# A five-stage LayerNorm whose scales are computed inside each stage, and the state space's output bias added beside the gates

## The chip, the cores and the metric

One Trainium2 chip; the kernel runs on one core. The metric is the device time of the whole kernel in microseconds; lower is better. Engines: PE is TensorE (matrix products), DVE is VectorE, ACT is ScalarE, POOL is GpSimd, SP issues transfers.

## The reference

An x of 16 x 64 tokens by 512 features goes through six blocks, each `x = x + block(layernorm(x))`; the layernorm has no weights:

```python
def _layernorm(x, axis=-1, eps=1e-05):
    m = jnp.mean(x, axis=axis, keepdims=True)
    v = jnp.var(x, axis=axis, keepdims=True)
    return (x - m) / jnp.sqrt(v + eps)
...
    x = x + _L0_xattn_ref(_layernorm(x, axis=-1), ctx_512, ctx_512, ...)   # 16 heads, 1601 keys a sequence
    x = x + _L0_attn_ref(_layernorm(x, axis=-1), ...)                      # state space, gate, output projection + b_out
    x = x + _L0_ffn_ref(_layernorm(x, axis=-1), ...)                       # router keeps 4 of 16 blocks a token
    x = x + _L1_xattn_ref(_layernorm(x, axis=-1), ctx_512, ctx_512, ...)   # one head, width 512
    x = x + _L1_attn_ref(_layernorm(x, axis=-1), ...)                      # causal self-attention
    x = x + _L1_ffn_ref(_layernorm(x, axis=-1), ...)                       # 4-bit weights, 16-bit activations
```

## The kernel before, in words

x lies in SBUF as eight tiles of 128 tokens by 512 (`NT` = 8, `x[:, t, :]`). The program is a row of stages, each a block of five instruction streams, one per engine; a stage begins on every engine when all have ended the one before. The stages are `cross0` (first cross-attention), `state_space`, `block_ffn`, `cross1_queries` and `cross1_batches` (second cross-attention), `self1`, and `quant_ffn`. Inside a stage the order of each engine's work is written out by hand, with semaphores between engines.

**The layernorm between stages.** Each of the first five blocks ends with an add per tile into x on VectorE, followed by that tile's statistics (`tile_stats`, L77: `bn_stats` into `k.stats`). When seven tiles are counted, and before the wait for the eighth tile's product, VectorE runs `norm_scales(0, 7)` (L82): seven `bn_aggr`, epsilon added, then 1/sqrt by an integer seed and three Newton steps of three small operations each, all on VectorE, and a last one for the shift -mean/sqrt. This stands in `cross0_batches` at L925, `state_space` at L1287, `block_ffn` at L1633, `cross1_batches` at L1904, `self1` at L2080. The next stage normalizes tiles at once (`hat_on_vector`, L187); after the fourth it runs `norm_scales` again for the eighth tile alone (`last_scales_on_vector`, L159; 14 operations). In `SharedNorm` (cross1_queries, self1) and in quant_ffn ScalarE normalizes tiles 4 to 7 from shift and scale. TensorE then turns each normalized tile (four transpositions into a PSUM bank, `turn_on_tensor`), and ScalarE or VectorE copies it out as xT. The norm at the very start of the program is another one (`small_on_vector`, L163, with the root on ScalarE, `root_on_scalar`, L210); its `loaded` is set.

**state_space.** VectorE: norm, then per tile the evictions of the projections; cumulative sums; a loop of 8 steps in which TensorE makes one product of the last eight Cm projections and one gate product a step, ScalarE evicts the projections and VectorE the gate (L1256; two banks); then 32 units (tile, head group). In unit n TensorE makes the decay and score products, ScalarE the exponential, VectorE `gated(n - 3)` (L1262) and `mixed(n)` (L1271, two operations), TensorE the products with the mixed matrix. In units 4 to 11 VectorE also adds the output bias `bO` to one tile of x (L1281). Last, eight output products (L1190), each added into x (L1289). GpSimd and SP, from the last gate on (`s_gT`), split the weights of block_ffn into two bf16 parts in 16 pieces (L1046, L1048) and store them.

The transfers of a stage's weights are issued by SP when the stage starts. In state_space TensorE waits for them before the first projections (`s_w`), in block_ffn after two turnings (`s_in`), in self1 before the queries and keys (`s_in`).

A table load of ScalarE (another set of functions for root, exponential, Silu or sigmoid) is put by the compiler directly ahead of the first activation that needs it, and ahead of that activation's wait.

## Time and profile before

| | us |
|---|---|
| three runs | 1679.1, 1680.76, 1686.83 (median 1680.76) |
| the profiled execution | 1682.18 |
| its span | 1680.5 |
| PE busy | 1549.7 (92%) |
| DVE busy | 1195.5 (71%) |
| ACT busy | 878.2 (52%) |
| POOL busy | 723.9 (43%) |

| stage | starts at, us into the span |
|---|---|
| cross0 | 0 |
| state_space | 854.7 |
| block_ffn | 995.4 |
| cross1_queries | 1212.5 |
| cross1_batches | 1238.1 |
| self1 | 1371.2 |
| quant_ffn | 1430.7 |

The profile's span is what the profiler saw between first and last instruction; the execution's own time lies 1.7 us above it. An engine's busy share says nothing of who waits: that is in the timeline, where a row gives the start, the length, the engine, the line, the operation and, in brackets, how long the engine had been idle before it and who ended that. Rows of one form that follow each other closely are merged (x2, x8).

### The profile page before, as it was taken

The page shows a single profiled execution, that of the slowest core. Times are in us where ns is not written, and L with a number is a line of the kernel's source. Part 1 is how long each engine was busy: PE and PEld are TensorE (multiplying, and loading weights), DVE is VectorE, ACT ScalarE, POOL GpSimd, SP SyncE. Part 2 cuts the span into 40 slices and gives each one's busy share as a digit, 9 for nine tenths or more (in the row PEclk, how much of TensorE's full clock was granted, in tenths as well). Part 3 has the DMA queues.
Part 4 walks back from the last instruction along what each step waited for, and adds up shares of the span by engine and source line. Part 5 has one row for each costly group of instructions (what it writes and reads, how often), then busy time and mean ns, then how long its engine had stood idle before and what let it go on. Part 6 is the DMA issues. An engine that isn't in the chain of part 4 may idle for free. (4 is left out here: it accounts for less than half of the span.)

```text
span 1680.5 us, 33759 instructions
## 1 busy us (share of the span) xinstructions
PE 1549.7 (92%) x13881; PEld 811.9 (48%) x13990; DVE 1195.5 (71%) x2049; ACT 878.2 (52%) x1176; POOL 723.9 (43%) x348
## 2 busy tenths in 40 slices
PE   6999999999999999999878889999889989899469
PEld 3445555555555555555453545344535544444134
DVE  6688888888888888888566558998832244527981
ACT  1387777777777777777544213431112221327650
POOL 1467888888887888876404832330000000000000
PEclk9999999999999999999989989999999999899779
DMA  3489999999999999999923644669699942000001
GB/s 139 126 181 194 186 195 191 189 199 185 196 189 199 190 194 188 188 201 166 195 87 107 222 167 150 158 165 213 177 421 416 377 181 127 1 0 1 0 1 51
DMA packets 554667, 282.02 MB, mean 168 GB/s; under 512 B 481664, under 2 KB 532608, under 8 KB 551440
## 3 DMA queue, kind: packets, MB, share of 16 engines
q1 hardware_dynamic: 554512, 279.84, 70.4%
q8 instruction: 111, 1.82, 0.4%
q14 instruction: 44, 0.36, 0.1%
HBM read 138.74 MB, written 22.54 MB: 96 GB/s over the span
## 5 line engine op out<-in xcount | busy, mean ns | idle before, releaser
L604 POOL TENSOR_TENSOR x<-x_prob,x 128x1604 bf16<-128x1604 f32 x120 | 387.9, 3232 | 144.0 <-ACT x L769 144.0
L899 DVE TENSOR_REDUCE x_negmax<-x_score 128x1 f32<-128x1604 f32 x128 | 233.7, 1826 | 17.5 <-PE x_score L645 7.3
L759 ACT ACTIVATE x_prob<-x_score,x_negmax 128x1604 f32<-128x1604 f32 x128 | 204.8, 1600 | 25.7 <-DVE x_negmax L899 21.0
L628 PE MATMUL x_ring<-x_ctx_hi,wk_split 128*128 128x400 bf16 (+1 forms) x1024 | 216.2, 333 | 0.3 <-DVE x_kT L827 0.3
L628 PE MATMUL x_ring<-wv_split,x_ctx_hi 128*128 128x512 bf16 (+1 forms) x770 | 200.3, 379 | 9.7 <-issue 6.9
L827 DVE SCALAR_TENSOR_TENSOR x_kT<-x_ring,bk,x_kT 128x400 bf16<-128x400 f32 (+1 forms) x256 | 162.3, 635 | 31.7 <-ACT x_kT L748 23.9
L769 ACT CAST x<-x_prob 128x1604 bf16<-128x1604 f32 x120 | 183.0, 1525 | 0.0
L833 DVE TENSOR_TENSOR x_v<-x_ring,x_v 128x512 bf16<-128x512 f32 (+1 forms) x208 | 143.8, 691 | 52.8 <-ACT x_v L752 50.0
L748 ACT ACTIVATE x_kT<-x_ring,bk 128x400 bf16<-128x400 f32 (+1 forms) x196 | 116.5, 594 | 90.7 <-PE x_ring L628 89.8
L752 ACT CAST x_v<-x_ring 128x512 bf16<-128x512 f32 (+1 forms) x148 | 86.7, 586 | 97.0 <-PE x_ring L628 97.0
L628 PEld LDWEIGHTS x_ring<-x_ctx_hi,wk_split 128*128 128x128 bf16 x1024 | 93.8, 97 | 87.0 <-issue 19.4
L2274 POOL MEMSET g_round<- 128x1 f32 x1 | 0.1, 98 | 300.8 <-POOLq L1927 300.8
L628 PE MATMUL x_ring<-x_ctx_lo,wk_split 128*128 128x400 bf16 (+1 forms) x512 | 128.4, 332 | 0.0
L628 PEld LDWEIGHTS x_ring<-wv_split,x_ctx_hi 128*128 128x128 bf16 (+1 forms) x832 | 77.4, 99 | 102.2 <-DVE x_kT L827 9.3
L661 PEld LDWEIGHTS x_pv<-x_pT,x_v 128*64 128x64 bf16 (+1 forms) x3328 | 97.6, 110 | 59.2 <-issue 58.5
L661 PE MATMUL x_pv<-x_pT,x_v 128*64 128x128 bf16 (+1 forms) x3328 | 118.3, 222 | 8.0 <-DMA x_pT<-x_kT 5.7
L2300 PE MATMUL g_bank<-g_x_split,g_w 128*128 128x512 bf16 x564 | 123.7, 379 | 1.4 <-DVE g_x_split L2413 0.8
L628 PE MATMUL x_ring<-wv_split,x_ctx_lo 128*128 128x512 bf16 (+1 forms) x415 | 123.5, 379 | 0.1
L553 POOL TENSOR_TENSOR x_ctx_lo<-x_stage,x_ctx_hi 128x802 bf16<-128x802 f32 (+1 forms) x64 | 106.1, 1658 | 30.2 <-DVE x_ctx_hi L808 28.9
L645 PE MATMUL x_score<-x_kT,x_q_rows 32*64 32x400 bf16 (+1 forms) x3072 | 91.6, 336 | 0.7 <-ACT x_prob L759 0.7
L546 POOL TENSOR_TENSOR x_ctx_hi<-x_stage,x_zero 128x800 bf16<-128x800 f32 (+1 forms) x60 | 91.2, 1521 | 0.3 <-DMA x_stage<-in_ctxT 0.2
L1435 PE MATMUL f_bank<-f_x_split,f_w 128*128 128x512 bf16 x374 | 89.3, 386 | 0.8 <-issue 0.4
(305 smaller groups left out, 2398.1 us busy)
## 6 DMA issues: line engine op xcount, KB each, us to landing
y_ctx<-in_ctx SPq DMA_DIRECT2D x16, 1664.0 KB, 12.3
y_ctxT<-in_ctxT SPq DMA_DIRECT2D x16, 1601.0 KB, 19.5
x_stage<-in_ctxT SPq DMA_DIRECT2D x48, 400.0 KB, 4.6
x_q_rows<-q_rows SPq DMA_DIRECT2D x64, 128.0 KB, 3.1
m_xT<-in_L_ffn_w SPq DMA_DIRECT2D x16, 512.0 KB, 4.6
ffn_w_parts<-m_xT SPq DMA_DIRECT2D x32, 256.0 KB, 2.7
x_stage<-in_ctxT SPq DMA_DIRECT2D x16, 401.0 KB, 4.7
f_w<-ffn_w_parts SPq DMA_DIRECT2D x4, 1024.0 KB, 8.4
```

What stands on the lines that cost most here:

```text
L553: pool.tensor_tensor(clo[:, :, at], stage[:, c % 2, :, 0:n], chi[:, :, at], ALU.subtract).then_inc(clo_done, 1)
L604: pool.tensor_tensor(ph[:, g % 2, 1, 0:NKP], prob[:, g % 2, :], ph[:, g % 2, 0, 0:NKP], ALU.subtract).then_inc(pl_done, 1)
L628: last = pe.matmul(out_, lhs, rhs, start=(i == 0), stop=(i == len(steps) - 1))
L645: last = pe.matmul(score[L * u:L * u + L, 512 * c:512 * c + w], qp[rows, par, a, hq, p // 2, :], kT[rows, par, hk, p // 2, QW * c:QW * c + w],
L661: last = pe.matmul(pv[L * h:L * h + L, 0:2 * L], v[0:kw, vpar, t, 2 * pp + h, :, :].rearrange("p s d -> p (s d)"), pT[0:kw, u, :, t, L * h ...
L748: nc.scalar.activation(kT[:, par, 0, m, n0:n0 + w], ring[g % RING][:, 0:w], ACT.Identity, bias=bk[:, KD * turned(c) + m:KD * turned(c) + m ...
L759: nc.scalar.activation(prob[:, g % 2, :].rearrange("p (c n) -> p c n", n=QW), scores, ACT.Exp, bias=nmax[:, g % 2:g % 2 + 1], accum_out=rs ...
L769: nc.scalar.copy(ph_of[g >= LAST][:, g % 2, 0, 0:NKP], prob[:, g % 2, :]).then_inc(ph_done, 1)
L827: dve.scalar_tensor_tensor(kT[:, par, 1, m, n0:n0 + w], ring[g % RING][:, 0:w], bk[:, KD * turned(c) + m:KD * turned(c) + m + 1], kT[:, pa ...
L833: dve.tensor_tensor(v[0:kw, par, m, :, 1, :], ring[g % RING][0:kw, :].rearrange("p (h d) -> p h d", h=H), v[0:kw, par, m, :, 0, :], ALU.su ...
L899: dve.tensor_reduce(nmax[:, pair % 2:pair % 2 + 1], scores, mybir.AxisListType.XY, ALU.max, negate=True).then_inc(max_done, 1)
L2300: last = pe.matmul(banks[2 + n % NB_G][:], wt[:, hw, j, m * P:(m + 1) * P], xs[:, hx, j, 512 * c:512 * c + 512], start=(i == 0 and j == 0) ...
```

## The change

Two things, and no others.

1. `norm_scales` is gone, and with it the scales of seven tiles at the end of a stage and of the eighth inside the next. The five stages after cross0 now begin as the norm at the start of the program does: `small_on_vector` on VectorE (eight `bn_aggr`, epsilon, reciprocal of ScalarE's root, four operations of one Newton step), with `root_on_scalar` on ScalarE; in `SharedNorm` and quant_ffn one more operation makes the shift of all tiles. The tiles are normalized after that. `tile_stats` stays where it was.
2. In state_space the eight adds of `bO` move from units 4 to 11 to the gate loop, one behind each gate's eviction.

The diff, cut:

```diff
-    def norm_scales(self, dve, first, last, step, base):
...
     def on_vector(self, dve):
+        self.small_on_vector(dve)
+        self.hat_on_vector(dve, range(NT))
+
+    def small_on_vector(self, dve):
+        before = NT if self.loaded else 0
         if self.loaded:
-            self.small_on_vector(dve)
-            self.hat_on_vector(dve, range(NT))
-        else:
-            self.hat_on_vector(dve, range(NT // 2))
-            self.last_scales_on_vector(dve)
-            self.hat_on_vector(dve, range(NT // 2, NT))
...
     def root_on_scalar(self, nc, act):
-        if not self.loaded:
-            return
         act.wait_ge(self.s_var, 1)
         nc.scalar.activation(self.small[:, 1, :], self.small[:, 0, :], ACT.Sqrt).then_inc(self.s_root, 1)
...
     def on_scalar(self, nc, act):
+        self.root_on_scalar(nc, act)
+        act.wait_ge(self.s_shift, 1)
         for t in range(self.HALF, NT):
-            if t == NT - 1:
-                act.wait_ge(self.s_var, self.LAST_SCALES)
             nc.scalar.activation(self.xhat[:, t, :], self.x[:, t, :], ACT.Identity, bias=self.shift[:, t:t + 1],
...
     def on_vector(self, dve):
+        self.small_on_vector(dve)
+        dve.scalar_tensor_tensor(self.shift[:], self.meanvar[:, :, 0], -1.0, self.rstd[:, :, 0], ALU.mult,
+                                 ALU.mult).then_inc(self.s_shift, 1)
         self.hat_on_vector(dve, range(self.HALF))
-        self.last_scales_on_vector(dve)
...
                 dve.tensor_scalar(gT[:, n // 2, 512 * (n % 2):512 * (n % 2) + 512], banks[4 + n % 2],
                                   bG[:, n // 2:n // 2 + 1], None, ALU.add).then_inc(s_gT, 1)
+                dve.tensor_tensor(x[:, n, :], x[:, n, :], bO[:], ALU.add).then_inc(s_xo, 1)
...
                 mixed(n)
-                if 4 <= n < 4 + NT:
-                    dve.tensor_tensor(x[:, n - 4, :], x[:, n - 4, :], bO[:], ALU.add).then_inc(s_xo, 1)
...
             for t in range(NT):
-                if t == NT - 1:
-                    k.norm_scales(dve, 0, NT - 1, s_stats, NT - 1)
                 dve.wait_ge(s_xo, NT)
...
+            norm.root_on_scalar(nc, act)
             for c in range(2):
                 for t in range(6 * c, 2 * c + 6):
                     norm.turned_on_scalar(nc, act, t)
```

The last piece is block_ffn's ScalarE. The call of `norm_scales` at the last tile goes in the same way in the four other stages, and quant_ffn's streams are changed as SharedNorm's.

**Where instructions stand now.** VectorE at the end of cross0 and the start of state_space, before (the add L932 is the last tile's, in two halves; L347 and L1220 are the branch between the stages):

```order
L845 TENSOR_TENSOR x<-x,x_stage 128x512
L88 BN_AGGR x_meanvar<-x_stats 128x2 x7
L91 TENSOR_SCALAR x_meanvar<-x_meanvar 128x7
...
L106 SCALAR_TENSOR_TENSOR x_shift<-x_meanvar,x_rstd 128x7
L932 TENSOR_TENSOR x<-x_ring,x 128x256 x2
L80 BN_STATS x_stats<-x 128x6
L347 UNCONDITIONAL_BRANCH
L1220 UNCONDITIONAL_BRANCH
L189 TENSOR_SCALAR m_xhat<-x,x_meanvar,x_rstd 128x512 x4
L88 BN_AGGR x_meanvar<-x_stats 128x2
```

and with the change:

```order
L809 TENSOR_TENSOR x<-x,x_stage 128x512
L894 TENSOR_TENSOR x<-x_ring,x 128x256 x2
L78 BN_STATS x_stats<-x 128x6
L312 UNCONDITIONAL_BRANCH
L1181 UNCONDITIONAL_BRANCH
L134 BN_AGGR m_meanvar<-x_stats 128x2 x8
L137 TENSOR_SCALAR m_small<-m_meanvar 128x8
L139 RECIPROCAL m_small<-m_small 128x8
L142 TENSOR_TENSOR m_small<-m_small 128x8
L144 TENSOR_TENSOR m_small<-m_small 128x8
L146 TENSOR_SCALAR m_small<-m_small 128x8
L148 TENSOR_TENSOR m_rstd<-m_small 128x8
```

The block between the seventh tile's add and the eighth's has gone; fourteen operations plus the root stand ahead of the first normalized tile. The same holds at the four other seams.

VectorE in state_space, gate loop and first units, before:

```order
L1252 TENSOR_SCALAR m_minus<-m_cum 80x512
L1256 TENSOR_SCALAR m_gT<-m_banks,m_bG 128x512 x8
L1271 TENSOR_TENSOR m_mix<-m_decay,m_banks 128x2x128 x6
L1262 TENSOR_TENSOR m_xhat<-m_banks,m_gT 128x128
L1271 TENSOR_TENSOR m_mix<-m_decay,m_banks 128x2x128 x2
L1262 TENSOR_TENSOR m_xhat<-m_banks,m_gT 128x128
L1271 TENSOR_TENSOR m_mix<-m_decay,m_banks 128x2x128 x2
L1281 TENSOR_TENSOR x<-x,m_bO 128x512
```

and with the change (the pair L1217, L1219 comes eight times):

```order
L1213 TENSOR_SCALAR m_minus<-m_cum 80x512
L1217 TENSOR_SCALAR m_gT<-m_banks,m_bG 128x512
L1219 TENSOR_TENSOR x<-x,m_bO 128x512
...
L1219 TENSOR_TENSOR x<-x,m_bO 128x512
L1233 TENSOR_TENSOR m_mix<-m_decay,m_banks 128x2x128 x6
L1224 TENSOR_TENSOR m_xhat<-m_banks,m_gT 128x128
L1233 TENSOR_TENSOR m_mix<-m_decay,m_banks 128x2x128 x2
```

The add stands behind each gate's eviction, and between a mixing and the next gated product nothing is left.

ScalarE in self1, before (L266 normalizes tiles 4 to 7, L2044 is the exponential):

```order
L266 ACTIVATE sn_xhat<-x,x_shift,x_rstd 128x512 x4
L270 COPY s_xT<-s_bank 128x4x128 x3
L2039 COPY s_v<-s_bank 128x512
L2044 ACTIVATE s_prob,s_stat<-s_sc,s_stat 128x128 x4
L2039 COPY s_v<-s_bank 128x512
```

and with the change:

```order
L176 ACT_TABLE_LOAD
L176 ACTIVATE sn_small<-sn_small 128x8
L229 ACTIVATE sn_xhat<-x,sn_shift,sn_rstd 128x512 x4
L233 COPY s_xT<-s_bank 128x4x128 x3
L1991 COPY s_v<-s_bank 128x512
L1996 ACT_TABLE_LOAD
L1996 ACTIVATE s_prob,s_stat<-s_sc,s_stat 128x128 x4
```

A load stands ahead of the root at the stage's start and another ahead of the first exponential. In the whole program ScalarE has 5 loads before and 13 with the change.

## Rows read from the trace of the kernel before

**Rows 1.** Timeline of VectorE, unit loop (start us, us, engine, line, operation, [idle before <- releaser]).
```profile
909.56 0.75 DVE L1271 TENSOR_TENSOR m_mix<-m_decay,m_banks 128x256 f32<-128x256 f32 x2 [0.81 <-PE m_banks L1179]
...
931.01 0.75 DVE L1271 TENSOR_TENSOR m_mix<-m_decay,m_banks 128x256 f32<-128x256 f32 x2 [0.46 <-PE m_banks L1179]
...
961.00 0.75 DVE L1271 TENSOR_TENSOR m_mix<-m_decay,m_banks 128x256 f32<-128x256 f32 x2 [0.81 <-PE m_banks L1179]
```

**Rows 2.** By line: two adds of one form (ns min/median/max, first and last start us).
```profile
L1281 DVE TENSOR_TENSOR x<-x,m_bO x8: 1517/1754/2147, 910.2 to 927.7; 128x512 f32<-128x512 f32 x8
...
L1730 DVE TENSOR_TENSOR x<-x,yq_bv x8: 681/687/689, 1220.1 to 1228.8; 128x512 f32<-128x512 f32 x8
```

**Rows 3.** Timeline of VectorE, last step of the gate loop.
```profile
900.44 0.75 DVE L1256 TENSOR_SCALAR m_gT<-m_banks,m_bG 128x512 f32<-128x512 f32 x1 [1.32 <-PE m_banks L1118]
```

**Rows 4.** Stretches: us, PE busy, PEld, DVE, ACT, POOL, granted clock, DMA share, GB/s.
```profile
862.00:864.00 2.00, 2.00 (x12) 2.00 (x11) 0.77 (x2) 0.43 (x1) 0.00 (x0) 0.50 0.89 278
...
880.00:900.00 20.00, 18.61 (x100) 4.44 (x96) 9.73 (x16) 14.38 (x24) 0.00 (x0) 1.00 0.00 1
```

**Rows 5.** Timeline, norm at the start of the program.
```profile
11.68 0.64 DVE L170 BATCH_NORM_AGGREGATE x_prob<-x_prob 128x2 f32<-128x6 f32 x8
...
12.73 0.21 ACT L214 ACTIVATE x_prob<-x_prob 128x8 f32<-128x8 f32 x1 [10.66 <-DVE x_prob L173]
...
14.02 3.74 DVE L189 TENSOR_SCALAR x_v<-x_v,x_prob 128x512 f32<-128x512 f32 x8
```

**Rows 6.** Timeline of ScalarE, a table load in state_space.
```profile
866.28 1.28 ACT L1198 ACT_TABLE_LOAD   x1
...
867.58 0.63 ACT L1198 ACTIVATE m_xn<-m_xb 128x512 f32<-128x512 f32 x1
```

**Rows 7.** Timeline, end of cross0 and start of state_space.
```profile
846.58 3.70 PE L679 MATMUL x_ring<-wo,catT 128*128 128x512 f32 x8
...
852.91 0.74 DVE L932 TENSOR_TENSOR x<-x_ring,x 128x256 f32<-128x256 f32 x2
...
854.68 0.33 SPq L1052 DMA_DIRECT2D m_wXA<-in_L_attn_WXA  x1
...
860.55 2.13 PE L1103 MATMUL m_banks<-m_wXA,m_xT 128*128 128x132 f32 x8 [2.94 <-DMA m_wG<-in_L_attn_WG]
```

**Rows 8.** Timeline, end of state_space and start of block_ffn.
```profile
975.53 16.90 PE L1190 MATMUL m_banks<-m_wO,m_xhat 128*128 128x512 f32 x39
...
993.66 0.68 DVE L1289 TENSOR_TENSOR x<-x,m_banks 128x512 f32<-128x512 f32 x1
...
995.36 0.39 SPq L1374 DMA_DIRECT2D f_router<-in_L_ffn_router_w  x1
...
1000.71 0.72 PEld L201 LDWEIGHTS f_bank<-ident,f_h 128*128 128x128 f32 x4 [3.14 <-DMA f_sel<-head_picks]
```

**Rows 9.** Timeline, start of cross1_queries (TensorE turns tiles 6 and 7).
```profile
1217.98 1.23 PE L258 MATMUL yq_bank<-ident,yq_xhat 128*128 128x128 f32 x8 [0.33 <-ACT yq_xhat L266]
```

**Rows 10.** Timeline, end of cross1_batches and start of self1.
```profile
1367.17 1.96 PE L1852 MATMUL y_wout<-y_wv,y_oT 128*128 128x512 f32 x4 [0.51 <-issue]
...
1369.20 0.68 DVE L1906 TENSOR_TENSOR x<-x,y_wout 128x512 f32<-128x512 f32 x1
...
1371.19 0.38 SPq L1961 DMA_DIRECT2D s_wq<-in_L_attn_Wq  x1
...
1378.27 0.30 PEld L1973 LDWEIGHTS s_bank<-s_xT,s_wq 128*128 128x128 f32 x2 [2.86 <-DMA s_wv<-in_L_attn_Wv]
```

**Rows 11.** Timeline, end of self1 and start of quant_ffn.
```profile
1425.86 0.58 DVE L88 BATCH_NORM_AGGREGATE x_meanvar<-x_stats 128x2 f32<-128x6 f32 x7
...
1428.98 0.74 DVE L2082 SCALAR_TENSOR_TENSOR x<-s_bank,s_stat,x 128x512 f32<-128x512 f32 x1
...
1430.77 1.92 DVE L189 TENSOR_SCALAR g_up<-x,x_meanvar,x_rstd 128x512 f32<-128x512 f32 x4 [0.32 <-PEq L1927]
...
1435.31 4.48 DVE L2402 TENSOR_REDUCE g_amax<-g_up 128x4 f32<-128x2048 f32 x2
```

More of the change, by code:

```diff
@@ L55, in __init__ @@
         self.used = []
-        self.stats = self.meanvar = self.rstd = self.shift = None
+        self.stats = None
         self.x = None
@@ L75, in sem, with tile_stats @@
         return self.used[-1]
-    def tile_stats(self, dve, x, t, done, counted):
+    def tile_stats(self, dve, x, t, done):
         dve.wait_ge(*done)
-        dve.bn_stats(self.stats[:, t, :], x[:, t, :]).then_inc(counted, 1)
-    def norm_scales(self, dve, first, last, step, base):
-        ve, r, u = self.meanvar[:, first:last, 1], self.rstd[:, first:last, 0], self.shift[:, first:last]
-        if base:
-            dve.wait_ge(step, base)
-        for t in range(first, last):
-            dve.bn_aggr(self.meanvar[:, t, :], self.stats[:, t, :]).then_inc(step, 1)
-        done = base + last - first
-        dve.wait_ge(step, done)
-        dve.tensor_scalar(ve, ve, EPS, None, ALU.add).then_inc(step, 1)
-        dve.wait_ge(step, done + 1)
-        dve.tensor_scalar(r.bitcast(I32), ve.bitcast(I32), 1, None, ALU.logical_shift_right).then_inc(step, 1)
-        dve.wait_ge(step, done + 2)
-        dve.tensor_scalar(r.bitcast(I32), r.bitcast(I32), -1.0, ROOT_SEED, ALU.mult, ALU.add).then_inc(step, 1)
-        done += 3
-        for _ in range(3):
-            dve.wait_ge(step, done)
-            dve.scalar_tensor_tensor(u, r, -0.5, r, ALU.mult, ALU.mult).then_inc(step, 1)
-            dve.wait_ge(step, done + 1)
-            dve.tensor_tensor(u, u, ve, ALU.mult).then_inc(step, 1)
-            dve.wait_ge(step, done + 2)
-            dve.scalar_tensor_tensor(r, u, 1.5, r, ALU.add, ALU.mult).then_inc(step, 1)
-            done += 3
-        dve.wait_ge(step, done)
-        dve.scalar_tensor_tensor(u, self.meanvar[:, first:last, 0], -1.0, r, ALU.mult, ALU.mult).then_inc(step, 1)
+        dve.bn_stats(self.stats[:, t, :], x[:, t, :])
     def keep_busy(self, pe, ident, bank, count):
@@ L129, in __init__ @@
         self.loaded = loaded
-        self.k = k
         if home is None:
-            self.meanvar, self.rstd = k.meanvar, k.rstd
+            self.stats = k.sb(ctx, name + "_stats", [P, NT, 6]) if loaded else k.stats
+            self.meanvar = k.sb(ctx, name + "_meanvar", [P, NT, 2])
+            self.rstd = k.sb(ctx, name + "_rstd", [P, NT, 1])
+            self.small = k.sb(ctx, name + "_small", [P, 4, NT])
         else:
@@ L146, in __init__ @@
         self.s_xT = k.sem(ctx, name + "_xT_done")
[L148 removed]
     def on_vector(self, dve):
+        self.small_on_vector(dve)
+        self.hat_on_vector(dve, range(NT))
+    def small_on_vector(self, dve):
+        before = NT if self.loaded else 0
         if self.loaded:
[L152 to L168 removed]
+            for t in range(NT):
+                dve.wait_ge(*self.loaded(t))
+                dve.bn_stats(self.stats[:, t, :], self.x[:, t, :]).then_inc(self.s_stats, 1)
+            dve.wait_ge(self.s_stats, before)
         for t in range(NT):
@@ L2322, in _ @@
         def _(act):
+            act.wait_ge(norm.s_var, 1)
+            nc.scalar.activation(norm.small[:, 1, :], norm.small[:, 0, :], ACT.Sqrt).then_inc(norm.s_root, 1)
+            act.wait_ge(s_shift, 1)
             for t in range(NT // 2, NT):
-                if t == NT - 1:
-                    act.wait_ge(norm.s_var, norm.LAST_SCALES)
-                nc.scalar.activation(xhat[:, t, :], x[:, t, :], ACT.Identity, bias=k.shift[:, t:t + 1],
+                nc.scalar.activation(xhat[:, t, :], x[:, t, :], ACT.Identity, bias=shift[:, t:t + 1],
                                      scale=norm.rstd[:, t, :]).then_inc(s_hat2, 1)
```

49 lines of the change are left out of this document (13 added, 36 removed).

## The prediction

> **What bounds the kernel now.** I read the busy shares first, then for each stage that the change touches the timeline around its start and end, and asked who waits for whom there. The first 854 us (cross0) run as before up to their last microseconds, so only five seams between stages and one loop are at stake.
>
> The loop is state_space's unit loop. From unit 13 on, two units' first mixings stand 1.765 us apart: (961.00 - 931.01) / 17 [rows 1]. There VectorE waits 0.81 us per unit for TensorE, so TensorE sets the pace. Between unit 4 (909.56) and unit 13 (931.01), where each of eight units carries one add of the output bias, nine units take 21.45 us in place of 9 x 1.765 = 15.88, and the idle time in front of the mixing is gone: there VectorE sets the pace. The add is why. It takes 1.5 to 2.1 us, while an add of the same form in cross1 takes 0.69 [rows 2]. In the unit loop GpSimd is splitting the next stage's weights nearly without a pause, and both of the add's sources lie in SBUF; in cross1 GpSimd is idle.
>
> At a seam the reader is to see two things: whether the last add of a stage starts when its product is there or only when the block of 7-tile scales is done, and what the first product of the next stage waits for.
>
> **The bias adds.** Out of the unit loop they give back 21.45 - 15.88 = 5.6 us. In the gate loop each follows a gate's eviction of 0.75 us, before which VectorE waits 1.32 us [rows 3]: the step is 2.07 us long, and 0.75 + 0.69 fits with 0.63 to spare. GpSimd is busy 0.00 us there [rows 4], so 0.69 is the price to take. Were it the 1.75 of the unit loop, the step would grow by 0.43 us, 3.4 us in eight; that is the bound above. The eighth add lies beside ScalarE's table load and first exponential. The block of splitting on GpSimd starts with the last gate, as before, and by the timeline its last stores are out while TensorE still works on the output products, so 5.6 us less do not uncover it. I take -5.6; from -5.6 + 3.4 = -2.2 to -6.
>
> **What replaces the scales.** Each of five stages now begins with all eight aggregates, one add, a square root on ScalarE behind a table load, a reciprocal and four small steps before its first normalized tile. The same chain at the start of the program takes 14.02 - 11.68 = 2.34 us, with the root 1.05 us after the first aggregate [rows 5]; the table was there long before. A load takes 1.28 us and the next activation follows 0.02 us behind it [rows 6]. The load stands ahead of the wait, so it starts with the stage and holds the root back to 1.3 us: 2.34 + 0.26 = 2.6 us to the first tile. In the three stages that share the tiles with ScalarE, one more small step makes 2.8: five of them fill 14.02 - 12.73 - 0.21 = 1.08 us [rows 5], 0.2 each. Below, nothing is shorter than 2.34; above, a load wholly in line gives 2.34 + 1.28 = 3.6. I take 2.6 and 2.8.
>
> The Trainium skill (ScalarE: Activation LUTs, section What ACT_TABLE_LOAD costs) puts a drain of about 1.38 us beside each load, 2.66 us per switch. No drain follows the load in rows 6; by that rule the first tile would come at 4.0.
>
> Three more loads, for the exponentials of block_ffn, cross1 and self1, have cover: softmax's mask is ready before TensorE comes to it, ScalarE is idle at the start of the batches, and in self1 TensorE turns the probabilities only after four products of values. Zero for these; if the cover were gone, 1.28 each. On ScalarE that makes eight loads more.
>
> **Seam A, cross0 to state_space.** The last product ends at 846.58 + 3.70 = 850.28, its add starts at 852.91 [rows 7], because the scale block stands ahead of it. Without the block it starts 0.1 behind the product: -2.5. The stage starts at 854.68, and its first projection waits until 860.55 for weights whose transfers start with the stage: 5.9 us. The new chain needs 2.6 to the first tile, 0.5 to write it (3.74 / 8 [rows 5]), at most 1.2 to turn it (two tiles take 1.23 at full clock [rows 9], so one takes as much at half) and at most 0.7 to copy it: 5.0 us, under 5.9. So the whole -2.5 stays, and its other bound is -2.5 + 1.3, should the chain take longer than the transfer by as much as a load.
>
> **Seam B, state_space to block_ffn.** The last product ends at 975.53 + 16.90 = 992.43, its add starts at 993.66 [rows 8]: -1.1. The third turning waits for a transfer until 1000.71, 5.35 us after 995.36. In the new order it also needs the first tile turned and copied twice: 2.6 + 0.5 + 1.2 + 1.2 = 5.5. I add 0.1: -1.0.
>
> **Seam C, block_ffn to cross1.** The last product of block_ffn is a long one, and its add already waits for it, so the block was hidden: 0 gained. At the start of cross1_queries, TensorE has nothing until the first tile, and its eight turnings lead straight to the products, with no transfer in the way. First tile +2.8; the wait of 0.33 us for tile 7, whose scales came late [rows 9], falls away: +2.4. In the batches TensorE never waits for the context, so nothing further on takes this back.
>
> **Seam D, cross1 to self1.** The last product ends at 1367.17 + 1.96 = 1369.13, its add starts at 1369.20 [rows 10]: the block ended just in time, 0 gained. The stage starts at 1371.19, and its first products wait until 1378.27 for a transfer, 7.1 us in. With the new chain the four tiles that they need are copied at 2.8 + 1.9 + 3 x 0.7 = 6.8: 0.
>
> **Seam E, self1 to quant_ffn.** Here the block is bare: it starts at 1425.86, when VectorE could have taken the last add, which starts at 1428.98 [rows 11]: -3.1. Then the peak of all tiles starts 1435.31 - 1430.77 = 4.5 us after the first tile; in the new order it follows four tiles (1.92) behind 2.8, at 4.7. Together -2.9.
>
> **Sum**: -5.6 - 2.5 - 1.0 + 2.4 + 0 - 2.9 = -9.6 us. The profiled execution took 1682.2 us, so 1672.6 in its terms; it lies 1.4 above the median of the three runs, 1680.8, so I predict 1671.2. About 0.5% (8.4 us) is what a measurement of this kernel tells from no change, so "faster" begins below 1672.4, hardly above my number.
>
> **Rivals.**
>
> *The load costs more than its row.* If ScalarE stays shut for as long again as the load lasted, 1.28 us, the first tile comes 1.3 later. Seam A then has 5.0 + 1.3 = 6.3 against 5.9 (+0.4), B, C and E take +1.3 each, D 8.1 against 7.1 (+1.0): +5.3, giving 1676.5. Against it stand rows 6; for it, that no row shows a load between a barrier and a root. The skill's drain, named above, is this rival, and would give much the same. Chance 0.10.
>
> *TensorE's clock.* It is at 0.50 of full, 1.2 GHz, when state_space's first projections run [rows 4], though TensorE is fully busy there; a wait of 2.94 us lies before them [rows 7]. In block_ffn too the turnings follow such a wait. The new chain makes the gap ahead of the turnings longer but nearly closes the one behind them, so the clock may come back sooner in A and B, and later in C. A tile's projections take 2.13 us at half clock [rows 7], of which full clock saves half: two tiles each in A and B give -4; two tiles' worth lost in C or E gives +2. That is 1667 to 1673. Chance of the gain 0.14; the loss lies within my range.
>
> *The start of a stage is bare everywhere.* If in A, B and D not the transfers but the new chain sets the first product (transfers land earlier, or turnings are slower than I take), the chain costs 2.6 + 2.6 + 2.8 + 2.8 + 2.8 = 13.6; against it stand 5.6 for the adds and 2.5 + 1.1 + 3.1 = 6.7 for the blocks: +1.3 us, 1682.1, slower. With 1.28 more at each, 1688.5. It decides from the point at which the first tile's copy ends after the transfer lands, 5.9 us into state_space. What speaks against it are the waits for transfers in rows 7, 8 and 10. Chance 0.06.
>
> *The adds do not leave the path.* If GpSimd's splitting or something else, and not VectorE, set the slow units, or the adds stretch the gates by 3.4, the -5.6 shrinks to 0 or -2.2: 1676.8 or 1674.6. The 0.81 us of idle that return as soon as the adds end speak against it. Chance 0.08.
>
> **How the numbers follow.** The forecast has 0.62 and an own range of 1667.5 to 1675: each seam is read to about 0.5 us, the run to run spread of 1679.1 to 1686.8 adds two. It splits 0.40 faster, 0.22 same. The rivals give 0.14 faster; 0.10, 0.08 and half of 0.06 same; the rest slower. So faster 0.54, same 0.43, slower 0.03. The range 1666 to 1677.5 takes in the clock's gain, the dear load and the stretched gates.
>
> **What would show it.** In the new profile the add with m_bO lasts 0.69 us and all units are 1.77 apart; the last adds of cross0 and self1 start within 0.2 of their product or of a free VectorE; the root follows the start of a stage by 1.3 us; the first projection of state_space still waits for its transfer; cross1_queries' first turning comes 3.4 us into its stage. A step of the gate loop over 2.1 us, a first tile later than 3 us, or a first projection released by a copy would prove me wrong in that term.

## The result, and the profile after

The changed kernel takes 1669.98 us (median of five runs, 1667.66 to 1672.3) against 1680.76 us before; the ratio is 0.9936, 95% interval 0.9919 to 0.9954. That is 10.8 us less, 7.7 to 13.6 by the interval. Forecast were 1671.2 us and 9.6 us less.

The two profiled executions lie 14.6 us apart (spans 1680.5 and 1665.9), because the one of before is among the longer of its runs and the one after the shortest of its own. Cut at the stages' starts, they show where the difference comes from:

| stretch | before, us | after, us | difference | forecast |
|---|---|---|---|---|
| cross0 to the end of its last product | 850.28 | 846.84 | -3.44 | 0, no edit there |
| from there to the start of state_space | 4.40 | 1.87 | -2.53 | -2.5 |
| state_space | 140.68 | 133.81 | -6.87 | -5.6 - 1.1 |
| block_ffn | 217.18 | 217.75 | +0.57 | +0.1 |
| cross1_queries | 25.53 | 27.29 | +1.76 | +2.4 |
| cross1_batches | 133.12 | 133.38 | +0.26 | 0 |
| self1 | 59.54 | 56.04 | -3.50 | -3.1 |
| quant_ffn | 249.77 | 248.92 | -0.85 | +0.2 |

(A stage's start is the issue of its first transfer, in quant_ffn GpSimd's first instruction; the end is the page's span, which is given to 0.1 us.) The first row is taken as scatter: in the thirteen profiles of this case the end of cross0's last product lies between 846.5 and 850.3 us, and TensorE's last wait for a transfer in cross0 is 5.49 us in the kernel before, 3.89 in the changed one and 4.92 in old_C, which ends cross0 as the changed one does. The three profiles with the old end of cross0 lie in the upper half, at 848.6 to 850.3, the ten with the new one at 846.5 to 848.8; that the edit has no part in this is not shown. Without that row the profiles differ by 11.2 us.

**Seam A.** Timeline of the changed kernel (start us, us, engine, line, operation, [idle before <- releaser]), end of cross0 and start of state_space, which answers to [rows 7]:

```profile
843.14 3.70 PE L643 MATMUL x_ring<-wo,catT 128*128 128x512 f32 x8
...
846.95 0.76 DVE L894 TENSOR_TENSOR x<-x_ring,x 128x256 f32<-128x256 f32 x2 [0.63 <-PE x_ring L643]
...
848.71 1.28 ACT L176 ACT_TABLE_LOAD   x1 [6.07 <-PEq L312]
...
850.00 0.21 ACT L176 ACTIVATE m_small<-m_small 128x8 f32<-128x8 f32 x1
...
851.29 3.74 DVE L153 TENSOR_SCALAR m_xhat<-x,m_meanvar,m_rstd 128x512 f32<-128x512 f32 x8
...
853.01 0.59 ACT L181 COPY m_xT<-m_banks 128x512 f32<-128x512 f32 x1 [2.80 <-PE m_banks L165]
...
853.87 0.59 ACT L181 COPY m_xT<-m_banks 128x512 f32<-128x512 f32 x1 [0.27 <-PE m_banks L165]
854.44 1.82 PEld L1064 LDWEIGHTS m_banks<-m_wXA,m_xT 128*128 128x128 f32 x8 [1.01 <-DMA m_wG<-in_L_attn_WG]
854.44 2.13 PE L1064 MATMUL m_banks<-m_wXA,m_xT 128*128 128x132 f32 x8 [0.61 <-ACT m_xT L181]
```

The last product ends at 843.14 + 3.70 = 846.84 and its add follows 0.1 later, where before it stood 2.6 behind [rows 7]. The load starts with the stage, at 848.71; the root follows at 850.00, 1.29 us in, and the first tile at 851.29, 2.58 in. The first projection starts 5.73 in, against 5.87 before. TensorE's row names the copy of the second tile, the weight loader's row the transfer of m_wG. It was the transfer: the first projection needs only the first tile, whose copy ends at 853.60, 0.84 us earlier, and the copy that TensorE's row names ends at 854.46, just behind the projection's start. The run own_waits below confirms it.

Stretches of the same kernel, the columns as in [rows 4]: the first projection, and a stretch that holds the third and those behind it.

```profile
854.44:856.56 2.12, 2.12 (x9) 2.12 (x10) 0.59 (x2) 0.01 (x1) 0.00 (x0) 0.50 0.79 156
...
858.70:868.00 9.30, 8.39 (x79) 7.96 (x84) 4.62 (x12) 7.29 (x13) 0.00 (x0) 1.00 0.21 80
```

TensorE's granted clock is 0.50 (1.2 GHz) at the first projection, as before, and 1.00 from 858.70.

**The bias adds.** Timeline of VectorE, a step of the gate loop and the mixings of two units; below, all adds by line (ns min/median/max):

```profile
881.87 0.75 DVE L1217 TENSOR_SCALAR m_gT<-m_banks,m_bG 128x512 f32<-128x512 f32 x1 [0.65 <-PE m_banks L1079]
882.53 0.68 DVE L1219 TENSOR_TENSOR x<-x,m_bO 128x512 f32<-128x512 f32 x1
...
910.48 0.75 DVE L1233 TENSOR_TENSOR m_mix<-m_decay,m_banks 128x256 f32<-128x256 f32 x2 [0.81 <-PE m_banks L1140]
...
912.25 0.75 DVE L1233 TENSOR_TENSOR m_mix<-m_decay,m_banks 128x256 f32<-128x256 f32 x2 [0.81 <-PE m_banks L1140]
```

```profile
L1219 DVE TENSOR_TENSOR x<-x,m_bO x8: 681/682/684, 880.5 to 895.0; 128x512 f32<-128x512 f32 x8
```

The add takes 0.68 us in every step. From the third mixing to the last of the 32 they stand 1.76 us apart, each behind a wait of 0.81 for TensorE.

**Seam B.** End of state_space, start of block_ffn ([rows 8] before):

```profile
957.82 22.91 PE L1151 MATMUL m_banks<-m_wO,m_xhat 128*128 128x512 f32 x53
...
980.84 0.69 DVE L1247 TENSOR_TENSOR x<-x,m_banks 128x512 f32<-128x512 f32 x1 [2.02 <-PE m_banks L1151]
...
988.32 1.12 PE L165 MATMUL f_bank<-ident,f_h 128*128 128x128 f32 x4 [0.64 <-DMA f_sel<-head_picks]
```

The product ends at 980.73, the add starts at 980.84, and the stage starts 1.1 us sooner behind the product than before (982.52 - 980.73 = 1.79 against 2.93). The third turning comes 5.80 us into the stage against 5.35.

**Seam C.** Start of cross1_queries ([rows 9] before):

```profile
1200.27 1.28 ACT L176 ACT_TABLE_LOAD   x1 [9.74 <-PEq L90]
...
1201.56 0.21 ACT L176 ACTIVATE yq_small<-yq_small 128x8 f32<-128x8 f32 x1
...
1202.93 1.91 DVE L153 TENSOR_SCALAR yq_xhat<-x,yq_meanvar,yq_rstd 128x512 f32<-128x512 f32 x4
...
1203.53 5.36 PE L221 MATMUL yq_bank<-ident,yq_xhat 128*128 128x128 f32 x32 [8.29 <-DVE yq_xhat L153]
...
1208.73 10.46 PE L1655 MATMUL yq_bank<-yq_xT,wqk 128*128 128x512 f32 x24
```

The root stands 1.29 us in, the first tile 2.66, the first turning 3.26 and the first product 8.46; before, that product stood 6.63 in. The 32 transpositions take 5.36 us here, at a mean granted clock of 0.67.

**Seams D and E.** self1's first queries ([rows 10]), and the last adds of self1 with quant_ffn's peak ([rows 11]):

```profile
1367.78 3.70 PE L1925 MATMUL s_bank<-s_xT,s_wq 128*128 128x512 f32 x8 [0.68 <-DMA s_wv<-in_L_attn_Wv]
```

```profile
1413.86 0.75 DVE L2032 SCALAR_TENSOR_TENSOR x<-s_bank,s_stat,x 128x512 f32<-128x512 f32 x1 [2.29 <-PE s_bank L1956]
1414.64 0.69 DVE L78 BATCH_NORM_STATS2 x_stats<-x 128x6 f32<-128x512 f32 x1
1415.25 0.73 DVE L2032 SCALAR_TENSOR_TENSOR x<-s_bank,s_stat,x 128x512 f32<-128x512 f32 x1
...
1421.67 4.48 DVE L2357 TENSOR_REDUCE g_amax<-g_up 128x4 f32<-128x2048 f32 x2
```

The queries start 6.84 us into self1 and wait for the transfer of s_wv, as before (7.08). The last add stands directly behind the statistics of tile 6, where before 3.1 us of small operations stood. The peak starts 4.69 us into quant_ffn, against 4.58.

### The profile page after: what moved, and what is told of

Read it like the earlier page. It is cut to its first block and busy times, and to the rows that moved or that the text cites. A ratio compares the mean times of both kernels' runs of the same rounds, so it can differ in the third digit from the quotient of the medians.

```text
span 1665.9 us, 33782 instructions
## 1 busy us (share of the span) xinstructions
PE 1558.5 (94%) x13990; PEld 809.1 (49%) x13990; DVE 1171.7 (70%) x1952; ACT 889.4 (53%) x1189; POOL 721.9 (43%) x348
## 5 line engine op out<-in xcount | busy, mean ns | idle before, releaser
L592 PE MATMUL x_ring<-wv_split,x_ctx_hi 128*128 128x512 bf16 (+1 forms) x832 | 214.2, 380 | 0.0
```

The costliest lines, as they stand in the source:

```text
L592: last = pe.matmul(out_, lhs, rhs, start=(i == 0), stop=(i == len(steps) - 1))
```

## The experiments

Each run gives a ratio to the kernel before, measured beside it, and a profile. Single executions of one kernel lie 2 to 10 us apart, so a single seam is read from the lengths of the stages:

| kernel | ratio, 95% interval | state_space | block_ffn | cross1_queries | self1 | quant_ffn |
|---|---|---|---|---|---|---|
| before | | 140.68 | 217.18 | 25.53 | 59.54 | 249.77 |
| changed | 0.9936 (0.9919-0.9954) | 133.81 | 217.75 | 27.29 | 56.04 | 248.92 |
| adds_only | 0.9968 (0.9955-0.9982) | 135.17 | 215.50 | 25.52 | 59.35 | 248.45 |
| scales_only | 0.9964 (0.9951-0.9978) | 139.48 | 216.99 | 28.02 | 56.60 | 251.25 |
| old_C | 0.9920 (0.9902-0.9938) | 134.15 | 217.23 | 25.52 | 59.30 | 248.59 |
| warm | 0.9932 (0.9914-0.9949) | 133.81 | 217.46 | 27.14 | 56.54 | 250.83 |
| more_loads | 0.9980 (0.9965-0.9995) | 134.61 | 217.40 | 29.90 | 57.28 | 253.19 |
| split_late | one run | 143.42 | 216.74 | 25.52 | 63.04 | 251.09 |
| own_waits | 0.9902 (0.9880-0.9923) | 131.77 | 215.90 | 27.53 | 55.69 | 251.51 |
| busy | 0.9912 (0.9891-0.9932) | 132.44 | 218.32 | 27.88 | 56.28 | 251.32 |
| changed_again | 0.9928 (0.9910-0.9947) | 134.01 | 216.85 | 27.82 | 55.98 | 249.12 |
| own_old | 0.9907 (0.9887-0.9928) | 131.66 | 217.91 | 25.51 | 55.68 | 251.27 |
| all_four | 0.9902 (0.9882-0.9922) | 131.27 | 217.43 | 25.52 | 55.30 | 249.24 |

**adds_only: the bias adds alone.**

```diff
@@ kernel before, state_space, VectorE
+                dve.tensor_tensor(x[:, n, :], x[:, n, :], bO[:], ALU.add).then_inc(s_xo, 1)
...
-                if 4 <= n < 4 + NT:
-                    dve.tensor_tensor(x[:, n - 4, :], x[:, n - 4, :], bO[:], ALU.add).then_inc(s_xo, 1)
```

> The kernel before with only the eight adds of the output bias moved into the gate loop; all scales stay as they were. Theory (VectorE paced units 4 to 12 because the add took 1.75 us beside GpSimd's splitting): 5.6 us faster than before, units 1.765 us apart throughout, the add 0.69 us, the gate step still 2.07. Rival (the scales made the whole difference, or the adds cost the gate loop what they give the unit loop): 0 to 2.2 us.

Measured: ratio 0.9968, 5.4 us less than before. state_space is 5.51 us shorter. The other stages have no edit, yet block_ffn, at 215.50, is the shortest of the thirteen profiles, 1.7 us under before, and quant_ffn is 1.3 us under before; no edit explains either. By line (ns min/median/max):

```profile
L1258 DVE TENSOR_TENSOR x<-x,m_bO x8: 680/681/681, 885.0 to 899.5; 128x512 f32<-128x512 f32 x8
```

The 5.6 us of the first term are there, and come from this edit alone.

**scales_only: the new norm alone.**

```diff
@@ changed kernel, state_space, VectorE
-                dve.tensor_tensor(x[:, n, :], x[:, n, :], bO[:], ALU.add).then_inc(s_xo, 1)
...
+                if 4 <= n < 4 + NT:
+                    dve.tensor_tensor(x[:, n - 4, :], x[:, n - 4, :], bO[:], ALU.add).then_inc(s_xo, 1)
```

> The changed kernel with the eight adds back in units 4 to 11; the new norm at the start of the five stages stays. Theory: seams A -2.5, B -0.7, C +1.8, D -0.2, E -3.1 and a little clock in quant_ffn, together 4 to 5 us faster than before, 5.6 us slower than the changed kernel. Rival (the adds are worth nothing): as fast as the changed kernel, 10.8 us faster than before.

Measured: ratio 0.9964, 6.1 us less than before (3.7 to 8.2 by the interval); 4 to 5 were expected. state_space is 1.20 us shorter than before, which is seam B's end without the adds. The two parts add up: 5.4 + 6.1 = 11.5 against 10.8 for the whole change, so neither hides the other.

**split_late: why the add was slow.** The kernel before, with one more wait on GpSimd.

```diff
@@ kernel before, state_space, GpSimd
             pool.wait_ge(s_gT, 2 * KD)
+            pool.wait_ge(s_xo, NT)
```

> The kernel before, its adds in units 4 to 11, but GpSimd's splitting of the next stage's weights begins only when the eighth add is done. Theory (the add is slow only because GpSimd works beside it): the add takes 0.69 us and nine units from unit 4 take 16 us in place of 21.45; the splitting then ends later than the stage's products, so the stage as a whole is longer, and block_ffn waits. Rival (the add is slow because of where it stands, or something other than GpSimd): it still takes 1.5 to 2.1 us.

Measured: all eight adds by line, then VectorE's timeline from the mixing of unit 4 to that of unit 13.

```profile
L1282 DVE TENSOR_TENSOR x<-x,m_bO x8: 682/684/686, 909.6 to 921.9; 128x512 f32<-128x512 f32 x8
```

```profile
908.90 0.75 DVE L1272 TENSOR_TENSOR m_mix<-m_decay,m_banks 128x256 f32<-128x256 f32 x2 [0.81 <-PE m_banks L1180]
909.57 0.68 DVE L1282 TENSOR_TENSOR x<-x,m_bO 128x512 f32<-128x512 f32 x1
...
924.78 0.75 DVE L1272 TENSOR_TENSOR m_mix<-m_decay,m_banks 128x256 f32<-128x256 f32 x2 [0.81 <-PE m_banks L1180]
```

At its old place, in the unit loop, the add takes 0.68 us once GpSimd is quiet, and nine units take 924.78 - 908.90 = 15.88 us, as the prediction had it for units without adds. The place was not at fault. The stage as a whole is 2.7 us longer than before, since the splitting, begun later, then ends last in it; the single run took 1688.6 us.

What happens in the collision is in the kernel before's timeline of unit 4 (GpSimd's L1046 and L1048 are the splitting):

```profile
909.36 1.90 POOL L1046 TENSOR_TENSOR m_xT<-m_xT,m_zero_col 128x1024 bf16<-128x1024 f32 x1
...
909.56 0.75 DVE L1271 TENSOR_TENSOR m_mix<-m_decay,m_banks 128x256 f32<-128x256 f32 x2 [0.81 <-PE m_banks L1179]
...
910.23 1.58 DVE L1281 TENSOR_TENSOR x<-x,m_bO 128x512 f32<-128x512 f32 x1
...
911.34 2.46 POOL L1048 TENSOR_TENSOR m_xT<-m_xT 128x1024 bf16<-128x1024 f32 x1
```

The add starts at 910.23, under a GpSimd operation that ends at 911.26, and lasts until 911.81, 0.55 us beyond that end. The same holds for all eight adds of this kernel:

| the add, start to end | GpSimd's running operation ends at | the add ends behind it by |
|---|---|---|
| 910.23 to 911.81 | 911.26 | 0.55 |
| 912.59 to 914.35 | 913.79 | 0.55 |
| 915.13 to 917.28 | 916.73 | 0.55 |
| 918.06 to 919.81 | 919.26 | 0.55 |
| 920.59 to 922.11 | 921.56 | 0.55 |
| 922.89 to 924.65 | 924.10 | 0.55 |
| 925.43 to 926.95 | 926.40 | 0.55 |
| 927.73 to 929.49 | 928.93 | 0.55 |

Whatever its length, an add ends at one distance behind GpSimd's operation. So it waits for that operation to finish; if both ran at half speed, the distance would vary. It works in the other direction too: GpSimd's next operation starts at 911.34, while the add still runs, and lasts 2.46 us, where in split_late this form takes 2.13 on average. The mixings, which have one of their two inputs in PSUM, take 0.75 us a pair beside GpSimd as without it. The Trainium skill (SBUF — State Buffer, section SBUF: two separate sides) has the rule: an operation of VectorE with two inputs in SBUF and a GpSimd operation that reads SBUF lock the same pair of ports, one for its whole length while the other is blocked. The rows above agree, with the one distance of 0.55 us in eight adds.

**old_C: seam C as before.** The functions `norm_scales` and the eighth tile's scales are taken back for this seam only.

```diff
@@ changed kernel, block_ffn and cross1_queries
+                if t == NT - 1:
+                    k.norm_scales(dve, 0, NT - 1, s_stats, NT - 1)
...
-        norm = SharedNorm(k, ctx, "yq", x, ident, banks[0:2] + banks[4:8], xT)
+        norm = SharedNorm(k, ctx, "yq", x, ident, banks[0:2] + banks[4:8], xT, early=True)
```

> The changed kernel with only the seam block_ffn to cross1_queries as before: seven tiles' scales under the last long product of block_ffn, the eighth's inside the stage, no root and no table load there. Theory (this seam alone loses): cross1_queries 25.5 us long in place of 27.3, 1.8 us faster than the changed kernel, so 12.6 us faster than before. Rival (a later wait takes it back, TensorE's clock or the batches' transfers): no faster than the changed kernel.

Measured: cross1_queries takes 25.52 us, as before, where the five profiles with the new chain and its one load have 27.3 to 28.0. The ratio is 0.9920, 2.7 us under the changed kernel's; the intervals overlap, so it is the stage's length that shows it. block_ffn did not grow (217.23): its end has more cover than the long product. In the kernel before, VectorE's last statistics end at 1209.40 and the last store of prepared weights lands at 1210.63; cross1_queries starts 1.9 us behind that landing, here and in eleven of the twelve other profiles. The profile would be faster still, had not self1 taken 59.30 us; its first queries, and the stretch in which they run:

```profile
1368.41 5.40 PE L1970 MATMUL s_bank<-s_xT,s_wq 128*128 128x512 f32 x8 [2.25 <-DMA s_wv<-in_L_attn_Wv]
```

```profile
1368.41:1371.90 3.49, 3.49 (x5) 1.48 (x6) 0.00 (x0) 0.00 (x0) 0.00 (x0) 0.62 1.01 437
```

The queries started behind the transfer of s_wv 8.40 us into self1, 1.6 later than in the changed kernel's profile, though nothing there differs; TensorE had waited 2.25 us, its clock in the stretch is 0.62, and the eight products take 5.40 us in place of 3.70 [rows 10].

**warm: the root's table already loaded.**

```diff
@@ changed kernel, end of ScalarE's work in cross0, state_space, block_ffn, cross1_batches, self1
+            nc.scalar.activation(k.warm[:], ident[:, 0:1], ACT.Sqrt)
```

> The changed kernel with a root of one column at the end of ScalarE's work in each of five stages, so that the table of the root is there when the next stage starts. Theory: the root follows the stage's start by 0.9 us (eight aggregates 0.64, the add 0.17, 0.05 between) in place of 1.3, so the first tile comes 0.4 us earlier; this is worth 0.4 each in cross1_queries and quant_ffn and nothing in state_space, block_ffn and self1, where a transfer ends last: 0.8 us faster than the changed kernel. Rival (the chain ends last at all five): 2.0 us faster. Rival (a load has a hidden cost after it, so the price seen is not all): more than 2.

Measured: timeline of cross1_queries, which starts at 1201.82, and of state_space's first projection (stage start 850.55).

```profile
1202.73 0.21 ACT L180 ACTIVATE yq_small<-yq_small 128x8 f32<-128x8 f32 x1 [9.17 <-DVE yq_small L141]
...
1204.10 1.91 DVE L157 TENSOR_SCALAR yq_xhat<-x,yq_meanvar,yq_rstd 128x512 f32<-128x512 f32 x4
```

```profile
856.47 2.13 PE L1069 MATMUL m_banks<-m_wXA,m_xT 128*128 128x132 f32 x8 [1.34 <-DMA m_wG<-in_L_attn_WG]
```

The root follows 0.91 us into the stage, the first tile 2.28: 0.38 earlier than in the changed kernel. In state_space the first projection still starts 5.92 in, released by the transfer, after 1.34 us of waiting in place of 0.61. cross1_queries is 0.15 us shorter, and in quant_ffn the first product of the hidden layer comes 15.19 in, against 15.57. Expected were 0.8 us in all; the ratio, 0.9932, cannot tell so little from nothing. The rival with five bare chains is out: in state_space, block_ffn and self1 a transfer released TensorE as before (5.92, 5.28 and 7.34 us in).

**more_loads: two table loads ahead of the root.**

```diff
@@ changed kernel, ScalarE, ahead of the root's wait in the five stages
+            nc.scalar.activation(k.warm[:, 0:1], ident[:, 0:1], ACT.Silu)
+            nc.scalar.activation(k.warm[:, 1:2], ident[:, 0:1], ACT.Sqrt)
```

> The changed kernel with an activation of one column from another table (Silu) and one from the root's table at the start of each of the five stages: two table loads ahead of the root in place of one. Theory (a load is its 1.28 us and an activation its 0.2, nothing hidden): the root waits until 1.28 + 0.2 + 1.28 + 0.2 = 3.0 us in, the first tile comes 1.7 us later; cross1_queries and quant_ffn grow by 1.7 each, state_space, block_ffn and self1, whose transfers land 0.5 to 1 us after the chain, by 0.9 to 1.7 each: 6 to 8 us slower than the changed kernel. Rival (each load leaves ScalarE shut for about as long again): the root at 5.5 us in, some 15 us slower.

Measured: ScalarE in cross1_queries.

```profile
1202.66 1.28 ACT L82 ACT_TABLE_LOAD   x1 [9.73 <-PEq L95]
1203.95 0.20 ACT L82 ACTIVATE warm<-ident 128x1 f32<-128x1 f32 x1
1204.16 1.28 ACT L83 ACT_TABLE_LOAD   x1
1205.45 0.20 ACT L83 ACTIVATE warm<-ident 128x1 f32<-128x1 f32 x1
1205.56 0.19 ACT L184 ACTIVATE yq_small<-yq_small 128x8 f32<-128x8 f32 x1
```

Load, activation, load, activation follow each other at 0.01 us; the root stands 2.90 us in. The ratio is 0.9980, 7.4 us above the changed kernel's (the medians lie 9.3 apart), and 6 to 8 were forecast. Part of that agreement is luck: cross1_queries grows by 2.6 and quant_ffn by 4.3 where 1.7 each were forecast, and TensorE's clock has its share in quant_ffn (last section); state_space grows by 0.8, self1 by 1.2, block_ffn not at all. What the run shows without luck is the timeline: each load has its own 1.28 us and nothing behind it.

**own_waits: TensorE waits only for what it uses.**

```diff
@@ changed kernel
-            sp.dma_start(wXA[:], d["L0_attn_WXA"]).then_inc(s_w, 16)
+            sp.dma_start(wXA[:], d["L0_attn_WXA"]).then_inc(s_wx, 16)
...
-            pe.wait_ge(s_w, 16 * 6)
+            pe.wait_ge(s_wx, 16)
...
-            sp.dma_start(wv[:], ...).then_inc(s_in, 16)
+            sp.dma_start(wv[:], ...).then_inc(s_wvin, 16)
...
-            pe.wait_ge(s_in, 48)
+            pe.wait_ge(s_in, 32)
```

TensorE waits for the other five weights of state_space ahead of the projections' last part, and for s_wv ahead of the values.

> The changed kernel with a semaphore of their own for the weights that the first projections of state_space need (m_wXA) and for those that self1's queries and keys don't need (s_wv), so that TensorE no longer waits there for transfers that it doesn't use yet. Theory (the transfer that lands last hides the new chain in these two stages by 0.5 to 1.5 us, no more): the first projection comes 5.1 us into state_space in place of 5.7 to 5.9, released by the copy of a tile, and self1's queries 6.4 us in place of 6.8 to 8.4; 1 to 2 us faster than the changed kernel, since the wait in self1 also lets TensorE's clock fall in some executions. Rival (the transfers were only beside the chain): no difference.

Measured: the first two projections (stage start 848.92), and self1's queries (stage start 1357.50).

```profile
853.95 1.94 PE L1066 MATMUL m_banks<-m_wXA,m_xT 128*128 128x132 f32 x8
...
856.16 1.07 PE L1066 MATMUL m_banks<-m_wXA,m_xT 128*128 128x132 f32 x8
```

```profile
1364.02 3.67 PE L1930 MATMUL s_bank<-s_xT,s_wq 128*128 128x512 f32 x8 [0.35 <-DVE s_xT L243]
```

5.03 us and 6.52 us in. So the chain, its turnings and copies would have allowed the first projection at 5.0 and the queries at 6.5, and the transfers covered them by 0.7 and 0.3 us in the changed kernel's profile. state_space gains 2.04 us, more than the 0.70 of the start: the second projection already runs in 1.07 us, at 2.4 GHz, 7.24 us in, where the changed kernel's took 1.84 at 8.51. The ratio is 0.9902, 5.7 us under the changed kernel's, with medians 2.5 us apart; the two stages explain 2.4, where 1 to 2 were expected.

**busy: idle products ahead of the turnings.**

```diff
@@ changed kernel, TensorE at the start of state_space, block_ffn, cross1_queries
+            k.keep_busy(pe, ident, banks[7], 10)
             norm.turn_on_tensor(pe, 0)
             norm.turn_on_tensor(pe, 1)
+            k.keep_busy(pe, ident, banks[7], 6)
```

The second group of six stands in state_space alone.

> The changed kernel with idle products on TensorE ahead of the first turning in state_space, block_ffn and cross1_queries (10 each, and 6 more before state_space's first projection). Theory (TensorE's clock is at 1.2 GHz in the first 10 us of state_space and 20 us of block_ffn because TensorE idled around the stage's start): at 2.4 GHz state_space's first two projections give back 2 us, block_ffn's routing and first products up to 5 us unless the weights' transfer then ends last: 3 to 7 us faster than the changed kernel. Rival (the clock stays where it is, or the transfers set the pace): within 1 us, or 1 us slower from the idle products standing before the turnings at half clock.

Measured: the first two projections of state_space (stage start 849.89), and two stretches of block_ffn (start 982.33), the columns as in [rows 4].

```profile
855.82 1.71 PE L1064 MATMUL m_banks<-m_wXA,m_xT 128*128 128x132 f32 x8
...
857.81 1.07 PE L1064 MATMUL m_banks<-m_wXA,m_xT 128*128 128x132 f32 x8
```

```profile
982.33:985.50 3.17, 1.25 (x10) 0.90 (x10) 2.37 (x16) 1.49 (x2) 0.82 (x2) 1.00 0.30 47
...
987.20:992.00 4.80, 3.91 (x20) 3.91 (x20) 3.35 (x7) 2.44 (x6) 0.00 (x0) 0.50 0.99 402
```

In state_space it works, the second projection takes 1.07 us and the stage 1.4 us less. In block_ffn the clock is 1.00 over the idle products, but 0.50 from 987.20 on, with TensorE busy in 3.91 of 4.80 us, and the stage is no shorter; in cross1_queries neither. The ratio is 0.9912, 4 us under the changed kernel's, of which the stages' lengths explain 1.4; expected were 3 to 7, and the expectation for block_ffn fell. Why the clock falls there was not tried further.

**changed_again, own_old, all_four.** own_old joins own_waits and old_C. all_four further adds warm's root ahead of state_space, block_ffn, self1 and quant_ffn, and the ten idle products ahead of state_space's turnings.

> The changed kernel itself, beside the two versions below on one chip, so that they can be compared with it directly. Expected: within 3 us of 1670, stages as long as in its first profile but for self1 and quant_ffn, which differ by up to 3 us from one execution to the next with the landing of a transfer and TensorE's clock.

> The changed kernel with the separate semaphores for the weights (state_space, self1) and, at the seam block_ffn to cross1_queries, the scales of the kernel before. Theory (the two gains lie in different stages and add up: 2.5 from the waits, 1.8 from the seam): 4.3 us faster than the changed kernel, about 1665.7. Rival (the gain of one is taken by what follows it): about 1667.5, as with the separate semaphores alone.

> The same, and also the root's table loaded at the end of the stages before state_space, block_ffn, self1 and quant_ffn, and ten idle products on TensorE ahead of state_space's first turning. Theory (with the transfers' waits gone the chain ends last in state_space and self1, so 0.4 us of a shorter chain now counts there and in quant_ffn: 1.2 us; TensorE's clock at 2.4 GHz for the turnings and the first projection: 0.5 to 1 us): 2 us faster than without, about 1664, 6 us faster than the changed kernel. Rival (the shorter chain changes nothing, since the clock or another transfer takes it back): as without.

Measured, on one chip: 1669.60, 1666.69 and 1664.97 us. The first projections of all_four (stage start 850.55):

```profile
855.23 1.79 PE L1113 MATMUL m_banks<-m_wXA,m_xT 128*128 128x132 f32 x8
```

4.68 us in. Its stages are together 5.6 us shorter than those of changed_again (state_space 2.7, cross1_queries 2.3, self1 0.7, quant_ffn 0.1 longer; block_ffn, 0.6 longer, and the batches left aside), and its median 4.6 us lower; 6 were expected. Its ratio to the kernel before is 0.9902 (0.9882 to 0.9922), that of changed_again 0.9928 (0.9910 to 0.9947), and the intervals overlap. Compared directly they do not: the six executions of all_four take 1663.7 to 1667.7 us, the six of changed_again 1667.8 to 1673.6. own_old lies between the two, 1.4 us short of what was expected of it; its quant_ffn was 2.2 us longer than changed_again's.

## Why the prediction was right, point by point

- **The bias adds, -5.6.** adds_only gives -5.5 in the stage and -5.4 in the whole. That GpSimd is the cause was read from two adds of one form [rows 2] and is now shown by split_late and by the one distance of 0.55 us in all eight adds. The gate loop had the room: the step is still 2.07 us, its wait fell from 1.32 [rows 3] to 0.65-0.72.
- **The chain, 2.6 and 2.8 us to the first tile.** It is 2.58 and 2.66. The load starts with the stage, and costs 0.38 us of the chain, not 1.28, because the aggregates run beside it (warm).
- **The dear load, rival.** It is out: no gap behind any load in more_loads, where loads stand in line. The Trainium skill (ScalarE: Activation LUTs, section What ACT_TABLE_LOAD costs) adds a drain of 1.38 us to the load's 1.28. The load's length agrees with the rows; no run here shows the drain.
- **Seam A, -2.5.** -2.53, and the first projection no later than before. The prediction named a first projection released by a copy as a sign of being wrong. TensorE's row does name a copy, but the first tile's copy had ended 0.84 us before the projection, so the transfer still ended last. The 5.0 us estimated for the new chain with turning and copy are 5.03 in own_waits.
- **Seam B, -1.0.** The end gives -1.1. The third turning was to be 0.1 later and was 0.45 later. In the twelve profiles with one load or none it lies 5.2 to 7.2 us in, and in every one the transfer of f_sel releases it, also with the norm of before (6.0 in adds_only) and at its latest in the last three (6.9 in changed_again, 7.2 in own_old, 7.1 in all_four). A tenth could not be read from one profile. The length of block_ffn does not follow it: 216.85 in changed_again, 217.75 in the changed kernel.
- **Seam C, +2.4.** +1.8 in the changed kernel's profile, +2.3 when it was profiled again, +2.0 to +2.5 in three others with that chain. The prediction counted one chain and one wait; what it left to its range is TensorE's clock in the turnings. In the changed kernel's profile they take 5.36 us at a mean granted clock of 0.67, in changed_again 5.90 at 0.61, in scales_only, the longest of the five, 6.10 at 0.58. This is the one seam that loses, and old_C takes the loss back.
- **Seam D, 0.** Nothing lost; the 0.24 us gained are the transfer's. The estimate of 6.8 us for the chain was 0.3 too long.
- **Seam E, -2.9.** self1 is 3.5 us shorter, of which 0.24 are seam D's, so -3.3 at its end; +0.1 at the peak.
- **The clock, rival.** The gain of 4 us did not come: the third projection is the first wholly at 2.4 GHz in both profiles, 10.6 us into state_space in place of 10.8, and in block_ffn the clock stays at 0.50 from the first turning until 19 us into the stage. What does move it in state_space is TensorE's waiting there (own_waits, busy).
- **The sum.** -9.6 forecast, -10.8 measured, -11.2 in the two profiles without cross0's row. The interval of the measurement, 7.7 to 13.6 us, holds the forecast. Against their forecasts quant_ffn is 1.0 us shorter in the profiles, cross1_queries 0.6, self1 0.4 and state_space 0.2, while block_ffn is 0.5 and the batches are 0.3 longer. quant_ffn and the batches have no edit that explains it, and block_ffn moves by more from profile to profile. That these partly cancel is luck; the agreement of the three large terms (-5.6, -2.5, -3.1), each read where it was forecast, is not.

## What to carry to other kernels

A block of small operations is worth its place ahead of a stage's last result only where the product behind it is long enough to hide it: of five seams here that held fully at two (block_ffn's end, cross1's end), while three ends were bare by 2.5, 1.1 and 3.1 us, and only cross1_queries had no cover for the new chain, so decide seam by seam by the wait that ends last on either side. An add with both inputs in SBUF belongs where GpSimd is quiet: 0.68 us there, 1.75 in the median beside the splitting 30 us further on. And where a transfer hides new work, ask whether the next instruction needs that transfer: two shared semaphores held back 0.7 and 0.3 us here, and a part of the clock's rise with them.
